# A fused decoder layer on one core: clearing the odd sums in three parts two steps later, and moving two more quarters of the K projection into the first three attention steps

## The chip, the cores and the metric

The kernel runs on one core of a Trainium2 chip. A core has a matrix engine (TensorE, PE in the profile, with PEld for its weight loads), a vector engine (VectorE, DVE), a scalar engine (ScalarE, ACT), a general engine (GpSimd, POOL), a queue engine (SyncE, SP) and 16 DMA engines. The metric is the device time of one execution in microseconds (us), smaller is better.

## The reference: what is computed

One decoder layer over 32 sequences (batches) of 128 rows and 256 features, float32:

```python
x = _layernorm(x + _L0_attn_ref(x, L0_attn_qkv_weights), axis=-1)          # causal self-attention, 16 heads of 16
x = _layernorm(x + _L0_xattn_ref(x, ctx_1024, ctx_1024, Wq, Wk, Wv), -1)   # retention with a decay mask on a context
x = _layernorm(x + _L0_ffn_ref(x, ...), axis=-1)                           # shared expert + 2 of 8 routed experts
```

In the self-attention, K is laid out in a peculiar way: `pre_k` of shape (rows, S, H, Dh) is turned to (Dh, S) per head after a plain reshape, so that one head's K mixes rows. The kernel therefore makes the K projection of eight sequences at a time (a group), writes it to device memory (`k_dram`) and reads each sequence's part back in the order in which the scores want it. In the routed part each row goes to the two experts with the largest gate probabilities, and the two results are added to the row.

## The kernel before

The engines run one program each, written out by hand, and meet at semaphores. There are three stages. The **front** (to about 28 us) loads x in four groups of eight sequences and makes the K projection. The **attention steps** follow: a function `step(n)` on each engine, for n from -2 on, where step n does the scores and the softmax of sequence n, the value product of sequence n-2, the cross part of n-3 and n-4, and the gate of n-5. Each step has the same work once the pipeline is full. The **tiles** (from about 470 us) run the routed experts over 71 tiles of 128 rows; each tile's result is added to one of two arrays in device memory, `totals[0]` (even tiles) and `totals[1]` (odd tiles), by an indirect DMA that adds. `totals[1]` has 33 x 128 rows of 256 floats and must be zero before the first odd tile.

What the change touches:

- **The K projection.** A group g has four quarters j. `project_k(g, j, bank)` on TensorE does a quarter as 8 matmuls into one PSUM bank (L735) and counts `k_made`; `out_k(g, j, bank)` on VectorE copies the bank to the group's place in `first_use` (L1304) and counts `kk_set`. Before the change the front holds groups 0 to 2 (12 quarters) and group 3 is spread: three quarters in step 0 and one in step 1. TensorE takes a bank again only after `kk_set` says that it was copied. The queue engine stores a finished group to `k_dram` (`store_k`, L453): group 0 in the front, groups 1 to 3 in its steps 1 to 3. K of sequence t comes back as eight loads in step t-1 (L477, `kp`).
- **What follows the front on TensorE:** `project(0)` (L768, L771: Q and V of sequence 0), the first masks (L778), then `scores(0)` (L791). `project(0)` waits for the x of sequence 0 (`xT_in`, issued at L467), for the small tables (`small_in`, L442 to L445) and others.
- **A step's inner order on TensorE (steps 0 to 2):** turning the probabilities of sequence n-1 (`turn_probs`, L803, four times, each needs the copy of the one before out of its bank: `out_probs`, on VectorE at L1434 or on ScalarE at L1112), the value product (`weigh`, L813), `scores(n)` (L791), `project(n+1)`. From step 3 on the cross part begins with L902, which needs the context of its sequence (`cT`, loaded at L486 in the step before).
- **The clearing.** GpSimd issues one DMA of zeros onto `totals[1]` at the start of its step 8 (L623), between two pieces of its own work: the root of the variance (L650) and the sum `kept` (L631). In steps 5 to 8 the queue engine also loads the routed experts' weights (L500, L503; four loads in a step). From step 12 on GpSimd sends each sequence's packets with two indirect DMAs a step (L637), after it has waited for the scores of the step.

Of the kernel before, what the change touches and what calls it, by code (L numbers as in the profile page):

```python
# [14 lines left out]
P = 128  # L15
# [22 lines left out]
EARLY = 4  # L38
SHARED_TURNS = 2
# [55 lines left out]
def decoder_kernel(nc, x, ctx_turned, wqkv, xwq, xwk, xwv, gate_w, gate_b, sw1, sb1, sw2, sb2,  # L95
                   rw1, biases, rw2, table_f32, table_bf16, x_turned, x_blocks, out):
    ctx = ExitStack()
    with ctx:
# [309 lines left out]
        def live(t):  # L408
            return 0 <= t < B
# [15 lines left out]
        def _(eng):  # L425
# [126 lines left out]
            eng.wait_ge(idle_sent, 48)  # L552
# [44 lines left out]
        def _(eng):  # L597
# [18 lines left out]
            def step(n):  # L616
# [5 lines left out]
                if n == 8:  # L622
                    eng.dma_start(totals[1][:, :].rearrange("(n p) d -> p n d", p=P),  # L623
                                  zeros[:, 0:D].unsqueeze(1).broadcast_to([P, B + 1, D])).then_inc(idle_sent, 16)
# [52 lines left out]
            eng.wait_ge(idle_sent, 48)  # L677
# [53 lines left out]
        def _(eng):  # L731
# [9 lines left out]
            for g in range(NG - 1):  # L741
                eng.wait_ge(xTu_in[g] if g else wk_in, 16)
                for j in range(4):
                    if g == 0:
                        eng.wait_ge(first_in[j], 16)
                    else:
                        eng.wait_ge(kk_set, (g - 1) * 4 + j + 1)
                    project_k(g, j, 4 + j)
            eng.wait_ge(xTu_in[NG - 1], 16)
            eng.wait_ge(ident_in, 16)  # L750
            eng.wait_ge(w_in, 32)
            eng.wait_ge(kk_set, 4 * NG - 5)
# [45 lines left out]
            def turn_probs(t, u):  # L798

                eng.wait_ge(expd, expd_count(t, u))  # L800
                after(eng, pT_set, t * 4 + u)
                for n in range(4):
                    mm = eng.transpose(PROBT[:, n * P:(n + 1) * P], prob[:, t % 2, 4 * u + n, :], ident)  # L803
                mm.then_inc(p_turned, 1)
# [69 lines left out]
            def step(n):  # L874
                if n == 1:
                    eng.wait_ge(kk_set, 13)
                if live(n - 1):
                    turn_probs(n - 1, 0)
                if n == 2:
                    eng.wait_ge(kk_set, 4 * NG)  # L880
# [4 lines left out]
                if n == 0:  # L885
                    eng.wait_ge(kk_set, 9)
                    project_k(NG - 1, 0, 4)
                if n == 1:
                    eng.wait_ge(kk_set, 14)
                    project_k(NG - 1, 3, 5)  # L890
# [51 lines left out]
                if live(n - 1):  # L942
                    turn_probs(n - 1, 2)
                t = n - 5
# [31 lines left out]
                if n == 0:  # L976
                    eng.wait_ge(kk_set, 12)
                    project_k(NG - 1, 1, 5)
                    project_k(NG - 1, 2, 7)
# [16 lines left out]
                if live(t):  # L996

                    eng.wait_ge(x1_set, t + 1)
                    after(eng, gc_set, n - 4)
                    for c in range(DC):  # L1000
                        mm = eng.transpose(TR[:, c * P:(c + 1) * P], x1[:, t % 2, c * P:(c + 1) * P], ident)
                    mm.then_inc(x1_turned, 1)
# [298 lines left out]
        def _(eng):  # L1301
# [5 lines left out]
            for g in range(NG - 1):  # L1307
                for j in range(4):
                    out_k(g, j, 4 + j)
# [158 lines left out]
            def step(n):  # L1468
# [7 lines left out]
                if n == 0:  # L1476
                    out_k(NG - 1, 0, 4)
                    lay_mask(1, 0)
                    lay_mask(1, 3)
                    out_k(NG - 1, 1, 5)  # L1480
                    out_k(NG - 1, 2, 7)
                if 0 < n <= SHARED_TURNS:
                    out_probs(n - 1, 1)
                if n == 1:
                    out_k(NG - 1, 3, 5)
                if n == 1:
                    out_probs(n - 1, 2)
                if live(t2):
                    eng.wait_ge(heads_turned, t2 + 1)
                    eng.reciprocal(rden[:, r2, :], HEADS[:, :, DH]).then_inc(den_set, 1)  # L1490
# [11 lines left out]
                if n == 2:  # L1502
                    out_probs(n - 1, 2)
# [253 lines left out]
```

## Time and profile before

| what | value |
|---|---|
| median of 3 runs | 726.83 us (725.86 to 726.84) |
| the profiled execution | 727.77 us, of which the span is 725.6 us |
| busy share of the span: PE, DVE, ACT, POOL | 94%, 67%, 66%, 47% |
| mean granted clock of TensorE | 0.986 |
| moved by DMA | 104.30 MB, mean 144 GB/s |

The profile is of one execution, which took 727.77 us, 2.17 us more than its span (start and end around it) and 0.94 us more than the median. Busy time says how much an engine worked, not whether the end waited for it; for that one reads the chain of work that ended last and the idle time before instructions. In the views, "PE ps L791" is TensorE writing to tile ps at line 791, and the bracket at the end of a row of the timeline is the idle time before it and what ended it. A row of windows has start:end and length, the busy time and instructions of PE, PEld, DVE, ACT and POOL, then the granted clock of TensorE (1.00 is 2.4 GHz, 0.50 is 1.2 GHz), the mean busy share of the DMA engines and GB/s.

### The profile page before, as it was taken

To read this page: it belongs to the slowest core of one execution; us is meant where nothing else is said; L and a number is where in the kernel's file an instruction comes from. 1 tells how busy PE (TensorE), PEld (TensorE's weight loads), DVE (VectorE), ACT (ScalarE), POOL (GpSimd) and SP (SyncE) were. 2 spreads that over 40 slices of the span, in tenths; PEclk is the share of its full clock that TensorE was granted. 3 is DMA by queue.
4 is the path that set the end of the run, shared out by engine and by line. 5 is a ranking of instruction groups with operands and counts; after the bars stand their busy time and mean duration, and the time that the engine had idled before them with its cause. 6 is when DMAs were issued, how large, how long until landed. Compare 5 with 4: busy or idle time off the path is not lost.

```text
span 725.6 us, 21537 instructions
## 1 busy us (share of the span) xinstructions
PE 682.8 (94%) x6174; PEld 589.5 (81%) x6175; DVE 489.3 (67%) x1563; ACT 478.6 (66%) x1319; POOL 341.7 (47%) x467
## 2 busy tenths in 40 slices
PE   7979999899999999999998889889999999999994
PEld 6868888788888888888887655779999999998653
DVE  3666877598888888888887456445555555555266
ACT  0278888588888888888885141356766666666246
POOL 1001334235454454554545446045656655556395
PEclk9999999899999999999999899999999999999998
DMA  8634469522332232323325224687777777776597
GB/s 314 216 131 138 140 198 308 194 61 76 91 94 70 89 100 75 107 80 107 112 80 173 76 72 147 186 220 132 139 133 142 135 139 134 141 135 133 118 349 264
DMA packets 93915, 104.30 MB, mean 144 GB/s; under 512 B 13168, under 2 KB 86640, under 8 KB 92944
## 3 DMA queue, kind: packets, MB, share of 16 engines
q1 hardware_dynamic: 78480, 79.43, 36.8%
q0 software_dynamic: 14656, 23.26, 16.8%
q8 instruction: 40, 0.66, 0.4%
q10 hardware_dynamic: 704, 0.66, 0.3%
q14 instruction: 35, 0.29, 0.1%
HBM read 62.21 MB, written 41.10 MB: 142 GB/s over the span
## 4 chain that ended last, share of the span: by engine, by line
PE 76%; DMA 6%; DVE 5%; SPq 4%; POOL 4%; issue 4%; ACT 1%; DVEq 0%; POOLq 0%; ACTq 0%
PE ps L1038 15%; PE ps L1047 8%; PE ps L803 6%; PE ps L902 5%; PE ps L791 5%; PE ps L768 4%; PE ps L813 4%; PE ps L905 4%; PE ps L735 4%; PE ps L926 4%; PE ps L771 4%; POOL first_use L711 2%; DMA xg<-sent 2%; PE ps L1025 2%; PE ps L823 2%
## 5 line engine op out<-in xcount | busy, mean ns | idle before, releaser
L1105 ACT ACTIVATE prob<-ps,nmax 128x128 f32<-128x128 f32 x512 | 146.5, 378 | 28.0 <-DVE nmax L1319 28.0
L1038 PEld LDWEIGHTS ps<-xgT,attn_only 128*128 128x128 f32 x1136 | 135.9, 192 | 7.4 <-DVE ghT L1600 1.8
L1038 PE MATMUL ps<-xgT,attn_only 128*128 128x128 f32 x1136 | 138.9, 276 | 1.1 <-ACT xgT L1217 1.1
L670 POOL DMA_INDIRECT total<-rot,result_row x71 | 112.4, 1583 | 35.3 <-issue 32.9
L1319 DVE TENSOR_REDUCE nmax<-ps 128x4 f32<-128x512 f32 x128 | 82.1, 685 | 17.9 <-PE ps L791 17.3
L1600 DVE SCALAR_TENSOR_TENSOR ghT<-ps,attn_only 128x128 f32<-128x128 f32 x142 | 43.3, 346 | 69.5 <-PE ps L1038 58.1
L613 POOL TENSOR_TENSOR rot<-products 128x128 f32<-128x128 f32 x128 | 61.1, 498 | 61.6 <-DVE products L1329 61.5
L1112 ACT COPY pT<-ps 128x512 f32<-128x512 f32 x124 | 74.3, 599 | 19.6 <-PE ps L803 15.3
L803 PE MATMUL ps<-tf,prob 128*128 128x128 f32 x512 | 78.5, 276 | 5.2 <-DVE pT L1434 4.2
L637 POOL DMA_INDIRECT sent<-packets,pos x64 | 63.4, 990 | 36.8 <-PE ps L791 22.6
L1047 PE MATMUL ps<-first_use,ghT 128*128 x284 | 74.5, 385 | 0.0
L803 PEld LDWEIGHTS ps<-tf,prob 128*128 128x128 f32 x512 | 59.1, 141 | 11.7 <-issue 4.1
L1225 ACT COPY attn_only<-first_use 128x512 f32 x71 | 44.0, 619 | 28.6 <-issue 28.6
L823 PE MATMUL ps<-prob,sw_sb 128*128 128x512 f32 x128 | 56.8, 594 | 0.0
L1217 ACT COPY xgT<-ps 128x256 f32<-128x256 f32 x71 | 26.4, 372 | 43.8 <-PE ps L1025 43.8
L1047 PEld LDWEIGHTS ps<-first_use,ghT 128*128 128x128 f32 x284 | 48.4, 190 | 5.4 <-issue 0.5
L1329 DVE TENSOR_TENSOR products<-ps,tf 128x256 f32<-128x256 f32 x128 | 46.4, 404 | 7.5 <-PE ps L905 2.3
L1589 DVE COPY attn_only<-first_use 128x512 f32 x71 | 31.2, 440 | 28.5 <-issue 28.0
L650 POOL TENSOR_TENSOR rstd<-mv,neg_half 128x1 f32<-128x1 f32 x32 | 17.6, 550 | 67.0 <-DVE mv L1337 67.0
L1211 ACT ACTIVATE attn_only<-ps,attn_only 128x128 f32<-128x128 f32 x142 | 44.1, 361 | 6.7 <-PE ps L1038 2.8
L658 POOL TENSOR_TENSOR weight<-weight_part,xg 128x1 f32<-128x1 f32 x71 | 13.3, 188 | 69.8 <-ACT rot L1231 52.9
L823 PEld LDWEIGHTS ps<-prob,sw_sb 128*128 128x128 f32 x128 | 23.9, 190 | 26.0 <-issue 25.6
(143 smaller groups left out, 1407.0 us busy)
## 6 DMA issues: line engine op xcount, KB each, us to landing
xg<-sent SPq DMA_DIRECT2D x71, 130.5 KB, 2.1
attn_only<-in_L_ffn_rb SPq DMA_DIRECT2D x71, 130.0 KB
first_use<-total SPq DMA_DIRECT2D x12, 512.0 KB, 8.5
total<-zeros POOLq DMA_DIRECT2D x1, 4224.0 KB, 18.0
k_dram<-first_use SPq DMA_DIRECT2D x4, 1024.0 KB, 5.1
attn_only<-in_x_turned SPq DMA_DIRECT2D x32, 128.0 KB, 2.3
attn_only<-k_dram SPq DMA_DIRECT2D x256, 16.0 KB
attn_only<-in_x SPq DMA_DIRECT2D x32, 128.0 KB, 2.7
```

Of the source, the lines that this page charges most:

```text
L613: eng.tensor_tensor(rot[:, t % 2, m + e, :], ra[:, t % 2, m + e, :], rb[:, t % 2, m + 1 - e, :], ALU.add).then_inc(done, 1)
L637: eng.indirect_dma_start(sent, bass.IndirectOffsetOnAxis(ap=pos[:, t, j:j + 1], axis=0), packets[:, t % SLOTS, :], None).then_inc(sent_in[ ...
L670: eng.indirect_dma_start(totals[slot % 2], bass.IndirectOffsetOnAxis(ap=result_row[:, slot:slot + 1], axis=0), yw[:, slot, :], None, compu ...
L803: mm = eng.transpose(PROBT[:, n * P:(n + 1) * P], prob[:, t % 2, 4 * u + n, :], ident)
L823: mm = eng.matmul(ps[:, bank + half, :].rearrange("p (b t) -> p b t", b=QB), sw1_sb[:, c, cols:cols + P], x2T4[:, q % EARLY, :, c, :], sta ...
L1038: mm = eng.matmul(ps[:, 2 * r + half, f * P:(f + 1) * P], w_now[:, r, c, cols:cols + P], xgT[:, r, c, :], start=(c == 0), stop=(c == DC - 1))
L1047: mm = eng.matmul(ps[:, 4 + r, 0:D], ghT[:, r, c, :], rw2_sb[:, bass.ds(e * (FFN // P * D) + c * D, D)], start=(c == 0), stop=(c == FFN // ...
L1105: ins = eng.activation(prob[:, t % 2, 4 * u + n, :], SCORE[u][:, n * P:(n + 1) * P], ACT.Exp, bias=nmax[:, t % 2, 4 * u + n:4 * u + n + 1])
L1112: eng.copy(pT[:, u, :, :].rearrange("p n t -> p (n t)"), PROBT).then_inc(pT_set, 1)
L1211: eng.activation(sil[:, r, f, :], ps[:, 2 * r, f * P:(f + 1) * P], ACT.Silu, bias=side[:, slot, f:f + 1]).then_inc(sil_set, 1)
L1319: eng.tensor_reduce(nmax[:, t % 2, 4 * u:4 * u + 4], SCORE[u].rearrange("p (h j) -> p h j", j=P), AX_X, ALU.max, negate=True).then_inc(max ...
L1329: eng.tensor_tensor(into[:, t % 2, m:m + 2, :], source, table[:, m:m + 2, :], ALU.mult).then_inc(done, 1)
```

## The change

First, the clearing of `totals[1]` is cut into three DMAs of 11 x 128 rows each, issued at the start of GpSimd's steps 10, 12 and 14, and no longer as one of 33 x 128 rows in step 8. Second, the front keeps 10 quarters of the K projection. The last two of group 2 and the four of group 3 are spread over steps 0, 1 and 2: three in step 0 as before (but other ones), two in step 1 (one before), one in step 2 (none before). Banks and counts of the waits are changed to fit.

```diff
+CLEARING = (10, 12, 14)
...
-                if n == 8:
-                    eng.dma_start(totals[1][:, :].rearrange("(n p) d -> p n d", p=P),
-                                  zeros[:, 0:D].unsqueeze(1).broadcast_to([P, B + 1, D])).then_inc(idle_sent, 16)
+                if n in CLEARING:
+                    many = (B + 1) // len(CLEARING)
+                    lo = CLEARING.index(n) * many * P
+                    eng.dma_start(totals[1][lo:lo + many * P, :].rearrange("(n p) d -> p n d", p=P),
+                                  zeros[:, 0:D].unsqueeze(1).broadcast_to([P, many, D])).then_inc(idle_sent, 16)
...
             for g in range(NG - 1):
                 eng.wait_ge(xTu_in[g] if g else wk_in, 16)
-                for j in range(4):
+                for j in range(4 if g < NG - 2 else 2):
...
-            eng.wait_ge(xTu_in[NG - 1], 16)
-            eng.wait_ge(kk_set, 4 * NG - 5)
+            eng.wait_ge(kk_set, 7)
...
                 if n == 1:
-                    eng.wait_ge(kk_set, 13)
+                    eng.wait_ge(kk_set, 12)
                 if live(n - 1):
                     turn_probs(n - 1, 0)
                 if n == 2:
-                    eng.wait_ge(kk_set, 4 * NG)
+                    eng.wait_ge(kk_set, 15)
...
                 if n == 0:
-                    eng.wait_ge(kk_set, 9)
-                    project_k(NG - 1, 0, 4)
+                    eng.wait_ge(kk_set, 8)
+                    project_k(NG - 2, 2, 7)
                 if n == 1:
+                    eng.wait_ge(kk_set, 11)
+                    project_k(NG - 1, 1, 7)
+                if n == 2:
                     eng.wait_ge(kk_set, 14)
-                    project_k(NG - 1, 3, 5)
+                    project_k(NG - 1, 3, 7)
...
                     turn_probs(n - 1, 2)
+                if n == 1:
+                    eng.wait_ge(kk_set, 13)
+                    project_k(NG - 1, 2, 5)
...
                 if n == 0:
-                    eng.wait_ge(kk_set, 12)
-                    project_k(NG - 1, 1, 5)
-                    project_k(NG - 1, 2, 7)
+                    eng.wait_ge(kk_set, 9)
+                    project_k(NG - 2, 3, 4)
+                    eng.wait_ge(xTu_in[NG - 1], 16)
+                    eng.wait_ge(kk_set, 10)
+                    project_k(NG - 1, 0, 5)
...
                 if n == 0:
-                    out_k(NG - 1, 0, 4)
+                    out_k(NG - 2, 2, 7)
                     lay_mask(1, 0)
                     lay_mask(1, 3)
-                    out_k(NG - 1, 1, 5)
-                    out_k(NG - 1, 2, 7)
+                    out_k(NG - 2, 3, 4)
+                    out_k(NG - 1, 0, 5)
                 if 0 < n <= SHARED_TURNS:
                     out_probs(n - 1, 1)
                 if n == 1:
-                    out_k(NG - 1, 3, 5)
-                if n == 1:
+                    out_k(NG - 1, 1, 7)
                     out_probs(n - 1, 2)
+                    out_k(NG - 1, 2, 5)
...
                 if n == 2:
+                    out_k(NG - 1, 3, 7)
                     out_probs(n - 1, 2)
```

In the changed kernel the same lines have other numbers: L735 is L739, L768 is L771, L803 is L806, L791 is L794 on TensorE; L1304 is L1317, L1319 is L1332, L1434 is L1447 on VectorE; L623 is L627 and L637 is L641 on GpSimd.

How TensorE's order changes, from behind `scores(1)` in step 1 to the turns of step 2 (a quarter is 4 matmuls in this order, and 8 records in the trace). Before:

```order
L735 MATMUL ps<-attn_only,first_use 128x256 x4
L803 MATMUL ps<-tf,prob 128x128 x12
L768 MATMUL ps<-attn_only 128x128 x4
L771 MATMUL ps<-attn_only 128x256 x2
L803 MATMUL ps<-tf,prob 128x128 x4
L813 MATMUL ps<-pT,va 32x128 x16
L791 MATMUL ps<-attn_only 128x128 x16
L912 MATMUL ps<-tf,oT 128x128 x4
L803 MATMUL ps<-tf,prob 128x128 x12
```

And now:

```order
L739 MATMUL ps<-attn_only,first_use 128x256 x4
L806 MATMUL ps<-tf,prob 128x128 x8
L739 MATMUL ps<-attn_only,first_use 128x256 x4
L806 MATMUL ps<-tf,prob 128x128 x4
L771 MATMUL ps<-attn_only 128x128 x4
L774 MATMUL ps<-attn_only 128x256 x2
L806 MATMUL ps<-tf,prob 128x128 x4
L816 MATMUL ps<-pT,va 32x128 x16
L794 MATMUL ps<-attn_only 128x128 x16
L739 MATMUL ps<-attn_only,first_use 128x256 x4
L918 MATMUL ps<-tf,oT 128x128 x4
L806 MATMUL ps<-tf,prob 128x128 x12
```

In step 1 the quarter behind the scores is still there (now another one), and a second quarter stands ahead of the last turn. In step 2 a quarter stands between the scores and the turning of the heads (L912, now L918), ahead of the three turns of the step.

VectorE's order in steps 1 and 2, from the maxima of step 1 (nmax) to the second copy of probabilities in step 2. "first_use<-ps" is `out_k`, "pT<-ps" is `out_probs`. Before:

```order
L1319 TENSOR_REDUCE nmax<-ps 128x4 [waits scored] x4
L1434 COPY pT<-ps 128x512 [waits p_turned]
L1304 COPY first_use<-ps 128x2x256 [waits k_made]
L1434 COPY pT<-ps 128x512 [waits p_turned]
L1428 CAST ps<-tb 128x512 [waits expd] x2
L1319 TENSOR_REDUCE nmax<-ps 128x4 [waits expd,scored] x3
L1434 COPY pT<-ps 128x512 [waits heads_made,p_turned]
L1490 RECIPROCAL rden<-ps 128x16 [waits heads_turned]
L1495 TENSOR_TENSOR att<-ps,rden 128x256 [waits den_set]
L1434 COPY pT<-ps 128x512 [waits heads_made,p_turned]
```

And now:

```order
L1332 TENSOR_REDUCE nmax<-ps 128x4 [waits scored] x4
L1447 COPY pT<-ps 128x512 [waits p_turned]
L1317 COPY first_use<-ps 128x2x256 [waits k_made]
L1447 COPY pT<-ps 128x512 [waits p_turned]
L1317 COPY first_use<-ps 128x2x256 [waits k_made]
L1441 CAST ps<-tb 128x512 [waits expd] x2
L1332 TENSOR_REDUCE nmax<-ps 128x4 [waits expd,scored] x3
L1447 COPY pT<-ps 128x512 [waits heads_made,p_turned]
L1503 RECIPROCAL rden<-ps 128x16 [waits heads_turned]
L1508 TENSOR_TENSOR att<-ps,rden 128x256 [waits den_set]
L1317 COPY first_use<-ps 128x2x256 [waits k_made]
L1447 COPY pT<-ps 128x512 [waits heads_made,p_turned]
```

One copy of a quarter was added behind the second pT of step 1, and one ahead of the second pT of step 2.

GpSimd's order where a part of the clearing now stands, in step 12 (step 14 reads the same, step 10 has no indirect DMAs):

```order
L654 TENSOR_TENSOR rstd<-mv,neg_half 128x1 [waits mv2_set]
L627 DMA total<-zeros 128x11x256
L635 TENSOR_TENSOR kept<-packets,sb_sb 128x256 [waits x2_set]
L641 DMA sent<-packets,pos 34688x261 [waits scored,pos_set]
L641 DMA sent<-packets,pos 34688x261
L615 TENSOR_TENSOR rot<-products 128x128 [waits scx_made,pk_set]
```

Before, the one clearing stood at the same place of step 8:

```order
L650 TENSOR_TENSOR rstd<-mv,neg_half 128x1 [waits mv2_set]
L623 DMA total<-zeros 128x33x256
L631 TENSOR_TENSOR kept<-packets,sb_sb 128x256 [waits x2_set]
L613 TENSOR_TENSOR rot<-products 128x128 [waits scx_made,pk_set]
```

The part is ahead of `kept` and of the two indirect DMAs of the step.

## Rows read from the trace of the kernel before

**Rows 1.** The page: the chain that ended last, by engine, share of the span

```profile
PE 76%; DMA 6%; DVE 5%; SPq 4%; POOL 4%; issue 4%; ACT 1%; DVEq 0%; POOLq 0%; ACTq 0%
```

**Rows 2.** Timeline of TensorE, steps 8 to 10 (start, length, line, idle before)

```profile
113.73 1.17 PE L791 MATMUL ps<-attn_only 32*128 32x128 f32 x32
...
125.50 1.18 PE L791 MATMUL ps<-attn_only 32*128 32x128 f32 x32 [0.58 <-issue]
129.59 2.07 PE L902 MATMUL ps<-attn_only 128*128 128x128 f32 x8 [2.91 <-DMA attn_only<-in_ctx]
...
142.52 1.17 PE L791 MATMUL ps<-attn_only 32*128 32x128 f32 x32
143.63 1.16 PE L902 MATMUL ps<-attn_only 128*128 128x128 f32 x8
```

**Rows 3.** Windows of 2 us: busy times, then granted clock, DMA share, GB/s

```profile
116.00:118.00 2.00, 2.00 (x16) 1.85 (x16) 1.51 (x5) 1.94 (x9) 0.00 (x0) 1.00 1.00 329
...
130.00:132.00 2.00, 2.00 (x10) 1.91 (x10) 0.00 (x0) 0.00 (x0) 0.00 (x0) 0.50 1.00 354
```

**Rows 4.** Windows of whole steps: step 7 with weight loads, step 14 without

```profile
102.55:113.73 11.18, 11.14 (x134) 9.74 (x131) 8.83 (x25) 9.45 (x29) 3.92 (x8) 1.00 0.63 202
...
187.22:198.33 11.11, 10.91 (x134) 9.79 (x130) 9.82 (x32) 9.45 (x29) 5.75 (x9) 1.00 0.33 85
```

**Rows 5.** The page: the clearing's issue, KB, us to landing

```profile
total<-zeros POOLq DMA_DIRECT2D x1, 4224.0 KB, 18.0
```

**Rows 6.** Timeline of GpSimd: its DMA issues and a send of step 14

```profile
113.41 1.92 POOL L623 DMA_DIRECT2D total<-zeros  x1
...
189.29 1.02 POOL L637 DMA_INDIRECT sent<-packets,pos  x1 [1.02 <-PE ps L791]
```

**Rows 7.** Timeline of the queue engine: loads in steps 8 and 10

```profile
112.55 7.71 SPq L477 DMA_DIRECT2D attn_only<-k_dram  x8
120.30 1.25 SPq L486 DMA_DIRECT2D attn_only<-in_ctx  x1
...
141.33 4.62 SPq L477 DMA_DIRECT2D attn_only<-k_dram  x8
```

**Rows 8.** Timeline of TensorE from the front to step 2

```profile
21.21 7.07 PE L735 MATMUL ps<-attn_only,first_use 128*128 128x256 f32 x32
28.12 1.05 PE L768 MATMUL ps<-attn_only 128*128 128x128 f32 x8
...
30.83 1.18 PE L791 MATMUL ps<-attn_only 32*128 32x128 f32 x32
...
43.97 0.63 PE L803 MATMUL ps<-tf,prob 128*128 128x128 f32 x4 [0.93 <-DVE pT L1434]
45.49 0.63 PE L803 MATMUL ps<-tf,prob 128*128 128x128 f32 x4 [0.89 <-DVE pT L1434]
...
51.06 0.60 PE L803 MATMUL ps<-tf,prob 128*128 128x128 f32 x4
53.12 0.63 PE L803 MATMUL ps<-tf,prob 128*128 128x128 f32 x4 [1.46 <-DVE pT L1434]
54.62 0.63 PE L803 MATMUL ps<-tf,prob 128*128 128x128 f32 x4 [0.87 <-DVE pT L1434]
```

**Rows 9.** Timeline of VectorE in steps 1 and 2

```profile
43.74 1.08 DVE L1304 COPY first_use<-ps 128x512 f32<-128x512 f32 x1
...
52.29 0.68 DVE L1434 COPY pT<-ps 128x512 f32<-128x512 f32 x1
...
53.78 0.69 DVE L1434 COPY pT<-ps 128x512 f32<-128x512 f32 x1 [0.19 <-PE ps L803]
```

**Rows 10.** The queue engine's x loads (L467): issue, and us to landing

```profile
L467 SPq DMA_DIRECT2D attn_only<-in_x_turned x2: 432/432/432, 19.9 to 20.4; - x2
...
DMA to landing us min/median/max: 5.3/5.4/5.4
```

**Rows 11.** Window of 1 us while K of sequence 0 lands

```profile
26.00:27.00 1.00, 1.00 (x6) 0.90 (x5) 0.41 (x1) 0.00 (x0) 0.00 (x0) 1.00 0.09 19
```

More of the change, by code:

```diff
@@ L38 @@
 EARLY = 4
+CLEARING = (10, 12, 14)
+assert (B + 1) % len(CLEARING) == 0
 SHARED_TURNS = 2
@@ L551, in _ @@
             eng.wait_ge(zeros_put, 16 * NE)
-            eng.wait_ge(idle_sent, 48)
+            eng.wait_ge(idle_sent, 16 * (2 + len(CLEARING)))
             def load(i, slot):
@@ L676, in _ @@
                 eng.wait_ge(x2_stored[r], 16 * (B - EARLY * QB) // 2)
-            eng.wait_ge(idle_sent, 48)
+            eng.wait_ge(idle_sent, 16 * (2 + len(CLEARING)))
             eng.wait_ge(kept_stored, 16 * EARLY)
@@ L998, in step @@
                     eng.wait_ge(x1_set, t + 1)
+                    if t == 0:
+                        eng.wait_ge(kk_set, 4 * NG)
                     after(eng, gc_set, n - 4)
@@ L1307, in _ @@
             for g in range(NG - 1):
-                for j in range(4):
+                for j in range(4 if g < NG - 2 else 2):
                     out_k(g, j, 4 + j)
```

## The prediction

> **What bounds the kernel now.** I read the chain of work that ended last first: TensorE has 76% of it [rows 1]. So time comes out only where TensorE waits or runs slowly, and the rest of the reading looks for such places near the two edits.
>
> The first is in steps 8 and 9. In TensorE's timeline scores(8) begins at 113.73, scores(9) at 125.50 and scores(10) at 142.52 [rows 2]: two steps take 28.79 us. Whole steps around them take 11.18 and 11.11 us [rows 4]. The excess is 28.79 - 11.18 - 11.11 = 6.50 us. Of it 0.58 + 2.91 = 3.49 us are idle time, ahead of scores(9) and ahead of the cross part, where the context's load had not landed. The other 3.0 us are slow running: the cross part's first group takes 2.07 us there and 1.16 in the next step [rows 2], and a window just behind the wait has a granted clock of 0.50, that is 1.2 GHz of 2.4, against 1.00 before [rows 3]. TensorE had sat idle 2.91 us ahead of that.
>
> Who made the load late? The clearing: 4224 KB, 18.0 us from issue to landing [rows 5], issued at 113.41 [rows 6], so the DMA engines were full until 131.4 (share 1.00, 329 GB/s) [rows 3]. The queue engine took 7.71 us to issue the eight K loads, against 4.62 in step 10, and came to the context only at 120.30 [rows 7]; TensorE could take it only at 129.59.
>
> The second place is the start. The front's last four quarters take 7.07 us of pure work at full rate, then project(0) begins at 28.12 and scores(0) at 30.83 [rows 8]. In steps 1 and 2 TensorE has idle gaps of 0.93, 0.89, 1.46 and 0.87 us, all for VectorE's copy of turned probabilities [rows 8]. These 4.15 us are the only room in which moved quarters could be hidden.
>
> **The change, part by part.** *The clearing leaves step 8.* With it goes the whole excess, if nothing else makes that load late: step 7 has the same weight loads as step 8, a DMA share of 0.63 and no excess [rows 4]. Term: -6.5. I take the slow clock with the wait, since its rows are at 0.50 only behind the wait.
>
> *Three parts arrive.* Each has 1408 KB. By 4224 KB in 18.0 us it needs 6.0 us, shared with other traffic; that was at 329 GB/s in all, and step 14 now moves only 85 GB/s, share 0.33 [rows 3 to 5]. The part starts, as the whole did, while the K loads are issued. If K loads are again issued over as much as 7.71 us instead of 4.62, the context's is issued as late in the step as it was in step 8; but the part has then about landed, and TensorE wants the context only 129.59 - 2.91 - 120.30 = 6.4 us later [rows 2, 7]. No wait. Bounds of each part: 0 below; above, a third of the old excess, 2.2 us. I take 0, as the row of the step with share 0.63 is nearer: with a part, step 14 moves 85 GB/s x 11.1 us + 1.44 MB = 2.4 MB, about step 7's 202 x 11.18 = 2.3 MB.
>
> *Issue on GpSimd.* A part costs GpSimd at most the whole's 1.92 us [rows 6], in front of `kept` and of the sends. In step 14 the sends wait 1.02 us for the scores [rows 6]; what is above that (at most 0.9) delays the rotation, whose result TensorE reads a step later. Cost 0. The two further issues have no waiter on TensorE. The last part is issued in step 14, and the first odd tile adds hundreds of us later.
>
> *The front ends two quarters earlier.* A quarter is (28.12 - 21.21)/4 = 1.73 us [rows 8], so TensorE is free 3.46 us earlier, at 24.66. But project(0) needs x of sequence 0: issued at 19.9, landing in 5.3 to 5.4 [rows 10], at 25.3. Its issue hangs on the first store of K, which doesn't move. So project(0), and with it scores(0), starts 28.12 - 25.3 = 2.8 earlier. Step 0 has as many quarters as before, at the same places. Then scores(0) needs K of sequence 0. Its eight loads are issued behind x, from about 20.8 on; at 4.62 us for eight [rows 7] the last goes out at 25.4, and if it lands as slowly as x, it is there at 30.8, and nothing of the 2.8 is left. The other bound: the engines are nearly idle from 26 to 27, share 0.09 [rows 11], so those loads had landed, and scores(0) can start at 28.0. I take that one, since it is a row on the loads themselves. Term: -2.8 (ends: -3.46 if x is in too, 0 if K lands as slowly as x).
>
> *Step 1 gets a quarter* ahead of the last turn, where TensorE idled 0.89 us [rows 8]. 1.73 - 0.89 = +0.8. VectorE's copy of it (1.08) [rows 9] lies behind the last copy of the step, where it next waits for scores(2). Term: +0.8.
>
> *Step 2 gets a quarter* behind the scores, ahead of the turn at 51.06. That turn ended at 51.66, 0.6 us before VectorE came to copy it, at 52.29 [rows 8, 9], so the copy starts 1.73 - 0.6 = 1.1 later. Then VectorE copies the quarter itself ahead of the second probabilities: 1.08, less the 0.19 that it idled there [rows 9]. TensorE's last turn waits for that copy. Term: 1.1 + 0.9 = +2.0. Here the quarter costs all it saved in front: TensorE's gaps of 1.46 and 0.87 [rows 8] were VectorE's work, and VectorE gets more of it.
>
> K projection: -2.8 + 0.8 + 2.0 = 0.0. Ends: -2.0 (step 2's quarter hides in TensorE's gaps after all) to +2.8 (K of sequence 0 is late). Sum: -6.5 + 0.0 = **-6.5**. The profiled execution took 727.77, so it would be 721.3; the runs' median is 0.94 below it, 726.83, which gives **720.3**.
>
> **A rule against the change.** The granted clock is 0.50 behind 2.91 us of idle time [rows 3], and 1.00 over whole steps that have no such wait [rows 4]. The Trainium skill, "TensorE: Matmul & The Clock Gate", section "HAM oscillation", says that a wait for a DMA that comes back again and again makes the array start cold each time, so that the cost of the clock is paid as often as there are waits. By that, three short waits would be dearer than one, if the parts make any; what it would give is the last rival. The trace agrees on the fall of the clock behind the one long wait.
>
> **The rivals.**
> 1. *The K quarters are hidden.* TensorE idled 4.15 us in steps 1 and 2, more than the 3.46 moved there. Against it: the gaps are VectorE's work, and step 2 adds a copy to it. The time then: -6.5 - 2.8 + 0.8 = -8.5, so 718.3.
> 2. *Parts still leave some waits*, because loads of K issued behind a part come late in each of three steps, without a fall of the clock: three times 0.58, the wait ahead of scores(9) [rows 2]. -6.5 + 1.7 = -4.8, so 722.0. For it: the K loads are issued together with the part, as then.
> 3. *The K move loses.* The queue engine's chain did not move while TensorE's did, so scores(0) waits for K of sequence 0: up to -6.5 + 2.8 = -3.7, 723.1; half of that, 721.7, is its middle. Against it: the quiet engines at 26 us [rows 11].
> 4. *Slower.* Each part makes the context's load late as the whole did, in steps 10, 12 and 14, and the clock falls each time: 3 x 6.50 in place of 6.50 is +13.0, so 739.8. It decides from the point where a part keeps the context's load from landing for more than a step, as 18.0 us did; 6.0 us end well ahead of that, so little speaks for it.
> 5. *The change doesn't do what it says*: the late load of step 8 was late for the weights of that step and not for the clearing. Then steps 8 and 9 keep their 6.5 and the result is 726.8. Against it: step 7 with the same loads is whole [rows 4].
>
> **How the numbers follow.** The forecast has 0.62; rival 1 0.12, rival 2 0.10, rival 3 0.09, rival 4 0.03, rival 5 0.04. The forecast's own spread is about 1 us to either side, 719.3 to 721.3. The range reaches over rival 1, rival 2 and most of rival 3: 718.2 to 722.6. About 0.2%, or 1.5 us, is what a measurement of this kernel can tell from no change. Faster than 725.4: the forecast and rivals 1 to 3, 0.93. Within 0.2%: rival 5, 0.04. Slower: rival 4, 0.03.
>
> **What the profile would show.** Scores begin every 11.1 to 11.2 us from step 7 to step 11, with a clock of 1.00 throughout and no idle time on TensorE for the context. Three clearing DMAs of 1408 KB, each landing in some 5 to 7 us. Project(0) starts at about 25.4, ahead of it a short wait for a DMA; scores(0) near 28.1. Step 1 and step 2 are longer by 0.8 and 2.0, so that scores(3) begins where it began before; in step 2 the last turn still waits for VectorE. It would be wrong if a part of the clearing holds up loads in step 10, 12 or 14, or if VectorE is not the one that TensorE waits for in step 2.

## The result and the profile after

The changed kernel takes 723.39 us (median of 22 runs, 720.01 to 728.08) against 728.26 for the kernel before on the same chip (22 runs, 724.45 to 730.97). The ratio is 0.9949, 95% interval 0.9932 to 0.9966. That is 3.7 us less (2.5 to 5.0), a gain clear of the noise but small, half a per cent, where 6.5 us were forecast. The time is 0.8 us above the top of the range. Part of that is the start of the sum: the three runs that gave 726.83 lay low, and 22 runs give 728.26. But 3.7 less than 726.83 is 723.1, which is outside too. The profiled execution took 723.76, its span is 721.7.

The page of the changed kernel: the span, the chain that ended last, and the issue of the three parts (count, KB, us to landing).

```profile
span 721.7 us, 21540 instructions
...
PE 78%; DVE 5%; DMA 5%; POOL 4%; issue 4%; SPq 3%; ACT 1%; DVEq 0%; POOLq 0%; ACTq 0%
...
total<-zeros POOLq DMA_DIRECT2D x3, 1408.0 KB, 8.0
```

TensorE's timeline in steps 8 to 10 of the changed kernel, which answers to [rows 2]:

```profile
114.98 1.17 PE L794 MATMUL ps<-attn_only 32*128 32x128 f32 x32
116.09 1.16 PE L908 MATMUL ps<-attn_only 128*128 128x128 f32 x8
...
126.10 1.17 PE L794 MATMUL ps<-attn_only 32*128 32x128 f32 x32
127.20 1.16 PE L908 MATMUL ps<-attn_only 128*128 128x128 f32 x8
...
137.21 1.17 PE L794 MATMUL ps<-attn_only 32*128 32x128 f32 x32
```

A step's length is the time from its scores to the next step's. Both waits are gone, and the cross part's first group takes 1.16 us where it took 2.07. Steps 8 and 9 last 22.23 us; before they lasted 28.79, so 6.56 went. The windows of whole steps 8 (weights alone), 10 and 12 (a part of the clearing each), which answer to [rows 3] and [rows 4]:

```profile
114.98:126.10 11.12, 10.92 (x135) 9.79 (x131) 8.73 (x25) 9.58 (x29) 3.66 (x7) 1.00 0.66 202
...
137.21:148.32 11.11, 10.92 (x134) 9.79 (x130) 9.83 (x32) 9.46 (x29) 4.71 (x8) 1.00 0.59 192
159.50:170.60 11.10, 10.90 (x142) 9.79 (x130) 9.53 (x28) 9.55 (x30) 6.60 (x10) 1.00 0.65 209
```

A step with a part has a DMA share of 0.59 or 0.65, no more than one with weight loads (0.66), a clock of 1.00 and a length of 11.11 or 11.10 us. The queue engine's loads in step 10 of the changed kernel (to [rows 7]):

```profile
136.02 6.40 SPq L479 DMA_DIRECT2D attn_only<-k_dram  x8
142.46 0.43 SPq L488 DMA_DIRECT2D attn_only<-in_ctx  x1
```

The K loads still take 6.40 us to issue beside a part (7.71 beside the whole, 4.62 alone), but the context goes out at 142.46, some 7 us before step 11's cross part.

TensorE from the front to step 2 (to [rows 8]):

```profile
21.82 3.62 PE L739 MATMUL ps<-attn_only,first_use 128*128 128x256 f32 x16
25.52 1.13 PE L771 MATMUL ps<-attn_only 128*128 128x128 f32 x8
...
28.31 1.17 PE L794 MATMUL ps<-attn_only 32*128 32x128 f32 x32
...
36.98 1.17 PE L794 MATMUL ps<-attn_only 32*128 32x128 f32 x32
...
47.37 1.17 PE L794 MATMUL ps<-attn_only 32*128 32x128 f32 x32
48.48 1.99 PE L739 MATMUL ps<-attn_only,first_use 128*128 128x256 f32 x8
...
52.22 0.63 PE L806 MATMUL ps<-tf,prob 128*128 128x128 f32 x4 [0.88 <-DVE pT L1447]
54.34 0.63 PE L806 MATMUL ps<-tf,prob 128*128 128x128 f32 x4 [1.49 <-DVE pT L1447]
54.80 1.72 PE L771 MATMUL ps<-attn_only 128*128 128x128 f32 x8
56.32 1.91 PE L774 MATMUL ps<-attn_only 128*128 128x256 f32 x4
...
59.99 1.17 PE L794 MATMUL ps<-attn_only 32*128 32x128 f32 x32
```

Project(0) starts at 25.52 and scores(0) at 28.31, 2.52 earlier than before. No wait stands ahead of project(0) in this profile, but x landed at about the same time as the front ended: the same kernel in e1, and three of the five others with this front, show a wait for it of 0.22 to 0.54 us. In e1:

```profile
25.09 1.13 PE L771 MATMUL ps<-attn_only 128*128 128x128 f32 x8 [0.54 <-DMA attn_only<-in_x_turned]
```

Step 1 takes 10.39 (9.74 before), step 2 takes 12.62 (9.41 before): +0.65 and +3.21. The two groups behind the gap of 1.49 take 1.72 and 1.91 us, where they took about 1.06 and 1.03 elsewhere. Windows of the changed kernel there:

```profile
52.00:54.00 2.00, 0.63 (x4) 0.42 (x4) 1.97 (x5) 1.06 (x4) 0.00 (x0) 1.00 1.04 311
54.00:56.00 2.00, 1.66 (x11) 1.69 (x12) 1.90 (x6) 0.59 (x1) 0.53 (x1) 0.75 0.38 131
56.00:58.00 2.00, 2.00 (x7) 1.56 (x7) 1.61 (x4) 1.14 (x4) 0.05 (x1) 0.50 0.03 8
```

TensorE is busy 0.63 of 2 us while it waits for VectorE, and behind that the granted clock is 0.75 and 0.50. VectorE of the changed kernel in step 2 (to [rows 9]):

```profile
51.38 0.69 DVE L1447 COPY pT<-ps 128x512 f32<-128x512 f32 x1 [0.89 <-PE ps L806]
...
52.61 1.06 DVE L1317 COPY first_use<-ps 128x512 f32<-128x512 f32 x1
53.52 0.68 DVE L1447 COPY pT<-ps 128x512 f32<-128x512 f32 x1
```

By this one pair of profiles the change would be worth 5.6 us up to scores(31) (371.83 against 377.42) and 3.9 at the end (721.7 against 725.6).

### The profile page after: what moved, and what is told of

Its sections match the earlier page's. It is cut to its first block, busy times and chain, and to the rows that moved or that the text cites. A ratio compares the mean times of both kernels' runs of the same rounds, so it can differ in the third digit from the quotient of the medians.

```text
span 721.7 us, 21540 instructions
## 1 busy us (share of the span) xinstructions
PE 683.2 (95%) x6174; PEld 588.5 (82%) x6175; DVE 489.2 (68%) x1563; ACT 478.9 (66%) x1319; POOL 343.1 (48%) x469
## 4 chain that ended last, share of the span: by engine, by line
PE 78%; DVE 5%; DMA 5%; POOL 4%; issue 4%; SPq 3%; ACT 1%; DVEq 0%; POOLq 0%; ACTq 0%
PE ps L1051 15%; PE ps L1060 8%; PE ps L806 6%; PE ps L908 5%; PE ps L794 5%; PE ps L816 4%; PE ps L771 4%; PE ps L739 4%; PE ps L911 4%; PE ps L774 4%; PE ps L932 4%; DMA xg<-sent 3%; POOL first_use L715 2%; PE ps L1038 2%; PE ps L826 2%
## 5 line engine op out<-in xcount | busy, mean ns | idle before, releaser
L1332 DVE TENSOR_REDUCE nmax<-ps 128x4 f32<-128x512 f32 x128 | 82.2, 685 | 17.7 <-PE ps L794 17.0
L806 PE MATMUL ps<-tf,prob 128*128 128x128 f32 x512 | 77.9, 275 | 4.4 <-DVE pT L1447 3.3
L641 POOL DMA_INDIRECT sent<-packets,pos x64 | 63.6, 993 | 35.6 <-PE ps L794 20.9
L806 PEld LDWEIGHTS ps<-tf,prob 128*128 128x128 f32 x512 | 58.7, 140 | 11.0 <-issue 4.9
```

The costliest lines, as they stand in the source:

```text
L641: eng.indirect_dma_start(sent, bass.IndirectOffsetOnAxis(ap=pos[:, t, j:j + 1], axis=0), packets[:, t % SLOTS, :], None).then_inc(sent_in[ ...
L1332: eng.tensor_reduce(nmax[:, t % 2, 4 * u:4 * u + 4], SCORE[u].rearrange("p (h j) -> p h j", j=P), AX_X, ALU.max, negate=True).then_inc(max ...
```

## The experiments

Sixteen runs were made, each with a profile, so that the stages can be told over many executions. Some repeat a kernel. Each ratio is to the kernel before on the same chip; e8, e10, e11 and e16 have one execution each and no ratio. "Old order" is TensorE's order of K quarters in the kernel before, "half clock" a granted clock of 0.50, and "excess" what steps 8 to 11 take above the 44.70 us that they take after the change.

**e1, the changed kernel again; e2, the clearing in parts alone** (the kernel before with GpSimd's lines of the change); **e3, the K quarters alone.**

```diff
# e3, in the changed kernel
-CLEARING = (10, 12, 14)
+CLEARING = (8,)
```

> The changed kernel once more, for a second profile and to share its chip with the single parts. Theory 1 (the clearing gives 6.5 us; the K move costs about 1.3 us, of which some 1.6 us is a stretch of half clock in step 2): ratio to before about 0.993; if the half clock in step 2 belongs to this order of work, this profile has it again (step 2 of about 12.6 us against 9.4 before). Rival (the half clock in step 2 was chance): step 2 of about 11.0 to 11.4 us and a clock of 1.00 there.

> Only the clearing is changed (three parts in steps 10, 12 and 14); the K projection stays as before. Theory 1: steps 8 and 9 take 22.2 us and not 28.8, so 6.5 us less than before, ratio about 0.991, and 1 to 1.5 us faster than the full change. Rival (the K move is neutral, and something behind the attention gives back what the result lacks): the same time as the full change, about 0.995.

> Only the K projection is moved; the clearing stays whole in step 8. Theory 1: scores(0) 2.5 us earlier, step 1 +0.65, step 2 +3.2, so scores(3) 1.3 us later than before: ratio 1.001 to 1.002. Rival (K move neutral as predicted): 1.000, scores(3) where it was; in that case step 2 has no half clock.

Ratios: e1 0.9935 (0.9907 to 0.9962), e2 0.9949 (0.9927 to 0.9971), e3 0.9999 (0.9975 to 1.0023). The 0.991 expected of e2 did not come; its rival's 0.995 did. All of the gain that can be told is the clearing's; moving the K quarters alone gives no difference (the interval reaches 1.8 us to either side). In e2 steps 8 to 11 take 44.69 us, as after the change (44.70), so the parts cost TensorE nothing. In e3, with the whole in step 8, they take 49.30: an excess of 4.60 and not 6.56. The repeats of the kernel before (e10, e16) show that this size differs between executions of one kernel: 5.89 and 4.40. Step 2 takes 12.33 in e1 and 12.62 in e3.

**e4, step 2's quarter in the gap**: TensorE does it while VectorE copies the first turned probabilities.

```diff
-                if n == 2:          # behind scores(n)
-                    eng.wait_ge(kk_set, 14)
-                    project_k(NG - 1, 3, 7)
...
+                if n == 2:          # behind turn_probs(n - 1, 1)
+                    eng.wait_ge(kk_set, 14)
+                    project_k(NG - 1, 3, 7)
```

> The full change, but in step 2 TensorE does its quarter of K behind the turn of the second four heads, and not ahead of it and of the turning of the heads; VectorE's order is as in the full change. Theory 1 (TensorE's quarter made VectorE idle 0.9 us, and long gaps on TensorE afterwards brought the half clock): step 2 takes about 10.4 us, 1.0 less from the order and 1.2 to 1.6 less from the clock, total about 2 us faster than the full change. Rival (VectorE's copy of the quarter alone sets step 2): step 2 unchanged at 12.6, or only the clock's part of it gone.

TensorE of e4 in step 2:

```profile
47.13 1.17 PE L794 MATMUL ps<-attn_only 32*128 32x128 f32 x32
...
49.38 1.89 PE L739 MATMUL ps<-attn_only,first_use 128*128 128x256 f32 x8
51.11 0.60 PE L806 MATMUL ps<-tf,prob 128*128 128x128 f32 x4
53.12 0.63 PE L806 MATMUL ps<-tf,prob 128*128 128x128 f32 x4 [1.41 <-DVE pT L1447]
53.58 1.06 PE L771 MATMUL ps<-attn_only 128*128 128x128 f32 x8
54.48 1.03 PE L774 MATMUL ps<-attn_only 128*128 128x256 f32 x4
```

Ratio 0.9897 (0.9868 to 0.9926). One gap of 1.41 is left, the groups behind it take 1.06 and 1.03, and the step 10.02 us instead of 12.62. The last turn begins 5.99 us behind the scores (6.97 after the change): 1.0 us is order, and 1.6 us is the clock, in this one profile.

**e5, the whole in step 10; e7, three parts in step 8.** Is it the place beside the weight loads, or the length of the one DMA?

```diff
# e5, in e2
-CLEARING = (10, 12, 14)
+CLEARING = (10,)
# e7, in e2
-                if n in CLEARING:
+                if n == 8:
...
+                    for lo in range(0, (B + 1) * P, many * P):
```

> K projection as before; the clearing is one DMA of 4224 KB again, but in step 10, where no weights are loaded. Theory 1 (it is the length of one transfer that holds up the context's load, the weights matter little): steps 10 and 11 take 4 to 6.5 us more than two whole steps, with a stretch of half clock; total about as before, ratio 0.998 to 1.000. Rival (it was the meeting with the weight loads of step 8, so that the move alone cures it): no excess, total as with three parts, ratio about 0.994 to 0.995. Beside it, tiles 10 to 70: 176.2 to 176.8 us if what stretches them is the later clearing, 175.1 to 175.7 if it is the number of clearing DMAs.

> K projection as before; three clearing DMAs of 1408 KB, all issued one behind the other in step 8. Theory 1 (the bytes in a row count, not the number of DMAs): steps 8 and 9 have the excess of about 5 to 6.5 us as before, ratio about 1.000. Rival (cutting alone helps, since the queue engine's loads slip in between): the excess falls below 3 us. Beside it, tiles 10 to 70: 176.2 to 176.8 us if the number of clearing DMAs stretches them, 175.1 to 175.7 if not.

TensorE of e5 in step 11, and then of e7 in step 9:

```profile
147.43 1.17 PE L795 MATMUL ps<-attn_only 32*128 32x128 f32 x32
150.57 1.16 PE L906 MATMUL ps<-attn_only 128*128 128x128 f32 x8 [1.97 <-DMA attn_only<-in_ctx]
```

```profile
126.33 1.17 PE L795 MATMUL ps<-attn_only 32*128 32x128 f32 x32 [0.84 <-issue]
130.24 2.07 PE L906 MATMUL ps<-attn_only 128*128 128x128 f32 x8 [2.73 <-DMA attn_only<-in_ctx]
```

Neither text on e5 was right: an excess came, but without the half clock. The whole away from the weights still makes the context late, by 1.97 us, but the clock stays up (1.16 behind the wait): the excess is 46.73 - 44.70 = 2.0 us, all of it the wait. That is one profile; whether the clock falls behind such a wait in other executions was not measured. Three parts issued together are the whole again: excess 6.63, ratio 1.0012 (0.9982 to 1.0042). So the gain has two parts: away from the weight loads, and steps between the pieces. The ratio of e5 is 0.9949 (0.9921 to 0.9976), the same as e2's: the 2 us lie within the two intervals, so only the trace shows them.

**e6 and e12, the quarter in the gap and copied by ScalarE; e8, the quarter where the change has it, but copied behind the second probabilities.**

```diff
# e6, e12, in e4
-                    out_k(NG - 1, 3, 7)      # VectorE, step 2
# and on ScalarE, between exps(n, 3) and out_probs(n - 1, 3)
+                if n == 2:
+                    eng.wait_ge(k_made, 16)
+                    eng.copy(kk_of(NG - 1).rearrange("p (a u) -> p u a", u=NU)[:, 6:8, :],
+                             ps[:, 7, :].rearrange("p (u a) -> p u a", u=2)).then_inc(kk_set, 1)
# e8, in the changed kernel, VectorE, step 2
-                    out_k(NG - 1, 3, 7)
                     out_probs(n - 1, 2)
+                    out_k(NG - 1, 3, 7)
```

> The full change, with two edits in step 2: TensorE's quarter of K behind the turn of the second four heads, and its copy done by ScalarE ahead of its own last copy of probabilities, where it waited 1.94 us, in place of VectorE. Theory 1: with both the quarter and the copy in idle time, step 2 takes 9.4 to 9.7 us as before the change, at full clock, so scores(3) comes 1.9 to 2.3 us earlier than before and the total is 8.5 us under it, ratio about 0.989. Rival (ScalarE is as tight as VectorE there): step 2 at 10.0 or more as with the move on TensorE alone.

> The full change, but in step 2 VectorE copies the quarter of K behind the second copy of probabilities and not ahead of it; TensorE's order is that of the full change. Theory 1 (VectorE's copy is what TensorE's last turn waits for, and the two gaps together bring the half clock): the last turn waits about 0.4 us in place of 1.49, no half clock in step 2, the step takes 11.0 to 11.4 us. Rival (TensorE's quarter ahead of the second turn alone sets the step): step 2 stays above 12 us.

> The version with TensorE's quarter of step 2 in the gap and its copy on ScalarE, once more, for a second profile and a second interval. If the first was no chance draw: steps 0 to 2 take 28.5 to 28.6 us at full clock again (the change itself had 31.4 to 31.7 in three profiles), steps 8 to 11 take 44.7, and the ratio to before is 0.989 to 0.993. Rival (the half clock in step 2 comes at random in every order of work, as it did in one profile of the kernel before): steps 0 to 2 take about 30 us in this profile.

TensorE of e6, and then of e8, in step 2:

```profile
52.49 0.63 PE L806 MATMUL ps<-tf,prob 128*128 128x128 f32 x4 [0.87 <-DVE pT L1451]
52.95 1.06 PE L771 MATMUL ps<-attn_only 128*128 128x128 f32 x8
```

```profile
52.17 0.63 PE L806 MATMUL ps<-tf,prob 128*128 128x128 f32 x4 [0.87 <-DVE pT L1447]
53.67 0.63 PE L806 MATMUL ps<-tf,prob 128*128 128x128 f32 x4 [0.88 <-DVE pT L1447]
54.13 1.06 PE L771 MATMUL ps<-attn_only 128*128 128x128 f32 x8
...
56.81 0.44 PE L1014 MATMUL ps<-tf,x 128*128 128x128 f32 x2 [0.76 <-DVE x L1538]
```

In e8 the copy no longer stands ahead of the last turn, the gap shrinks from 1.49 to 0.88 (0.4 was expected) and the clock stays up, but `x` is late by 0.76: 11.31 us. In e6 and e12 step 2 takes 9.49 and 9.48 and is as short as without a quarter. Ratios: e6 0.9921 (0.9894 to 0.9948), e12 0.9895 (0.9858 to 0.9933); e8's one run took 723.51. These kernels are the best: e4, e6 and e12 beat the kernel before and, by the middle of their intervals, the change; only e4's interval is clear of the change's.

**e9, two small DMAs more; e10, the kernel before; e11, e2 again.** In e2 and after the change the stretch of the tiles (from the tenth to the seventieth) was 0.8 to 1.0 us longer than before. Do more DMAs on GpSimd's queue do that?

```diff
# e9, in the kernel before
+                if n in (12, 14):
+                    lo = (n - 12) // 2 * P
+                    eng.dma_start(spare[lo:lo + P, :], zeros[:, 0:D]).then_inc(idle_sent, 16)
```

> The kernel before, with two more small DMAs (128 KB of zeros each onto unused rows of device memory) issued by GpSimd in steps 12 and 14; the clearing stays whole in step 8. Theory (the tiles' stretch comes with two more DMAs on GpSimd's queue, wherever they are and however large): tiles 10 to 70 take 176.2 to 176.8 us in place of 175.1 to 175.8, and the total is about 1 us above before, ratio 1.001. Rival (it comes with the clearing of the odd sums in parts): tiles 10 to 70 at 175.1 to 175.8, ratio 1.000.

> The kernel before once more, for a second profile of it. If the parts of the time that the change does not touch are the same from one execution to another, scores(31) begins 346.6 us behind scores(0), tile 0 some 84.3 us behind scores(31), and tiles 10 to 70 take 175.1 to 175.8 us. If they vary by 1 to 2 us, then that is what stands between the 5.6 us gained by scores(31) and the measured ratio.

> Only the clearing in three parts once more, for a second profile, since the first was of the fastest of its executions. Up to scores(31) it should be the same as the first (6.5 us less in steps 8 and 9, and no excess); tiles 10 to 70 at 176.2 to 176.8. An execution of 724 to 725 us should show its longer time behind scores(31): in the passage to the tiles, in tiles 0 to 10 or at the end.

The theory fell: that stretch is 176.35 in e9 and 177.64 in e11, but 176.58 in e10, the kernel before (175.74 in its first profile). e9's ratio is 1.0003 (0.9979 to 1.0026). The same profiles showed something else. TensorE of e10 in step 2, in the old order:

```profile
53.38 0.63 PE L803 MATMUL ps<-tf,prob 128*128 128x128 f32 x4 [1.45 <-DVE pT L1434]
54.88 1.09 PE L803 MATMUL ps<-tf,prob 128*128 128x128 f32 x4 [0.87 <-DVE pT L1434]
55.76 1.92 PE L768 MATMUL ps<-attn_only 128*128 128x128 f32 x8
57.47 1.28 PE L771 MATMUL ps<-attn_only 128*128 128x256 f32 x4
```

The same gaps as in [rows 8], 1.45 and 0.87, and this time the clock falls behind them. The kernel before pays this too, in some executions.

**e13 to e16: is the gain given back behind scores(31)?** With the three parts alone steps 8 to 11 are 4.4 to 6.6 us shorter than with the whole, but the ratio of e2 gives only 3.7. Theories A to D are in the text of e13 and e14.

```diff
# e13, in e2; spare has as many rows as totals[1]
+                if n == 8:
+                    eng.dma_start(spare[:, :].rearrange("(n p) d -> p n d", p=P),
+                                  zeros[:, 0:D].unsqueeze(1).broadcast_to([P, B + 1, D])).then_inc(idle_sent, 16)
# e14, in e2: in project(t), ahead of its own six matmuls
+                for _ in range(3 if t == 10 else 0):
...              # the same six matmuls, without a signal
```

> Three parts of the clearing in steps 10, 12 and 14, and besides them GpSimd writes as many zeros (4224 KB) as the old clearing into a spare array at the old place in step 8: work that the reference does not ask for. Steps 8 and 9 should again be some 5.7 us longer (mean of five profiles of kernels with the whole there). The question is the stretch behind scores(31): 348.6 us in the mean of four profiles with the clearing whole in step 8 (347.7 to 349.8), 351.4 in the mean of nine with it moved (349.0 to 353.2). Theory A, a stall in step 8 makes the later stretch short: it is short again here, and the mean span is that of the kernel before (725 to 726). Theory B, writing the real array later makes the later stretch long: it stays long, some 351.4, and the mean span is 2.7 above that of the kernel before. Theory C, the difference of the two groups of profiles is chance: the mean span is that of the three parts alone (722.0) and 5.7, 727.7, and the stretch is anywhere from 348 to 353.

> Three parts of the clearing in steps 10, 12 and 14, and in step 9 TensorE does the projection of sequence 10 four times instead of once (three times of work whose result is overwritten with the same values), about 3 x 1.8 = 5.4 us of work without idle time. Theory D, the stretch behind scores(31) depends on when it begins: it begins as late as in the kernel before, is short, and the mean span is 725 to 726. Theories A, B and C: busy work changes nothing later, so the mean span is 722.0 + 5.4 = 727.4.

> Three parts in steps 10, 12 and 14 and nothing else, a third time. If the stretch behind scores(31) is longer with the clearing moved, it is above 349.8 again (it was 349.0 and 353.2) and the ratio is near 0.995, not the 0.991 that the traces up to scores(31) would give. If that was chance, the stretch is as often near 348 as near 353, and the ratio comes nearer 0.992.

> The kernel before, for one more profile of the stretch behind scores(31): 347.7 to 349.8 if kernels with the clearing in step 8 have it short, anywhere up to 353 if not. Steps 8 to 11 take 49 to 51.5 us.

Ratios: e13 1.0020 (0.9994 to 1.0045), e14 1.0027 (1.0009 to 1.0045), e15 0.9967 (0.9939 to 0.9995). All eighteen profiles in the order in which scores(31) begins (us; "whole" means 4224 KB written in step 8):

```
kernel  scores(31)  behind it      kernel  scores(31)  behind it
e6        368.89     349.91        e15       373.42     350.18
e4        369.12     352.38        e13       375.45     349.65  whole
e12       369.18     352.92        e3        376.86     348.64  whole
e2        370.27     349.03        before    377.42     348.18  whole
e8        370.52     351.08        e16       377.72     348.38  whole
e11       370.87     353.23        e9        377.84     352.46  whole
e1        371.28     351.12        e7        377.86     347.74  whole
after     371.83     349.87        e14       378.10     347.90
e5        373.33     352.27        e10       378.32     349.78  whole
```

The stretch behind scores(31) is 349.3 us in the mean of the seven with the whole in step 8 and 350.9 in the eleven others. The line through the eighteen falls by 0.29 us for each us that scores(31) begins later (correlation -0.58; 7 of 1,000 random orders of the same numbers are as steep). So the profiles give back some 1.6 us on the way to the end.

The experiments do not say through what. B is not favoured: e14, with the clearing moved and the time filled with work, has a short stretch, 347.90. A is not borne out: e13, with its stall, has 349.65 and a mean span of 726.4, between A and C, and e9 has 352.46. D has its direction right by its profile, but not by its time. The mean spans that the theories named assume the 725.8 that the kernel before had in the first runs; it has 724.9 beside e14, whose ratio is 1.0027, and its interval is above the 1.000 that D gives and holds the 1.002 of the others. So C, chance alone, is not excluded.

Where the 1.6 us lie can be read: 0.5 before the first tile and 1.1 from there on. A part of it is the clock. The time lost to it behind scores(31), one less the granted clock times the length of each 1 us window, is 5.6 to 6.6 us in six of the seven with the whole (9.8 in e9), 5.7 to 9.6 in the ten with it moved and no filler, and 4.4 in e14. In the mean of the seven and of the eleven that is 6.5 and 7.0, so the clock is 0.4 of the 1.6, and the rest has no cause found.

## Why the prediction was wrong in size, part by part

**The clearing leaves step 8, -6.5.** Right in mechanism: waits, slow rows and the late context all went, and e7 brought them back. But less than half of it is the clearing by itself: in step 10, away from the weight loads, the whole cost 2.0 us (e5). Wrong in size. The rows of [rows 2] came from an execution near the top: steps 8 to 11 of the seven profiles with 4224 KB in step 8 (before, e3, e7, e9, e10, e13, e16) take 51.26, 49.30, 51.33, 49.60, 50.59, 49.14 and 49.10, mean 50.05, against 44.68 to 44.72 in those with the parts in steps 10, 12 and 14 and no filler. The term is -5.35.

What made it too large is above all the slow running, which the prediction put at 3.0 us. Summed over windows of 1 us, the clock costs 3.4 us in steps 8 to 11 of before, e7 and e10 and 1.7 us in the other four; the waits differ less. A window of 12 us around the wait in the kernel before, first in the profile that the prediction read, then in e16 (granted clock 0.72 and 0.86):

```profile
126.00:138.00 12.00, 8.83 (x65) 7.92 (x60) 4.70 (x12) 4.57 (x15) 1.70 (x4) 0.72 0.89 306
```

```profile
126.00:138.00 12.00, 9.48 (x110) 8.25 (x108) 6.51 (x18) 6.63 (x19) 2.74 (x6) 0.86 1.02 356
```

Of the 3.35 us that the clearing gained by leaving the weight loads, an estimate from these rows and e5 is that 2.4, the mean of the seven, are clock.

**Three parts, 0.** Right: 11.11 us a step at a clock of 1.00. The parts land in 7.8 to 8.0 us in this profile (medians of 6.8 to 8.3 in the others with parts in steps 10, 12 and 14) and not in 5 to 7, but nothing on TensorE waited for it. Rival 4, which the prediction's paragraph on the rule calls the last and which the clock rule of the Trainium skill ("TensorE: Matmul & The Clock Gate", "HAM oscillation") stood beside, did not come: there was no wait to come back. Rival 2's waits of 0.58 did not come either, nor rival 5.

**The front, -2.8.** Right: -2.52 in the pair of profiles; in the mean 28.22 in three against 30.94 in the eleven of the old order, -2.7. The forecast bound, the landing of `x`, is there as a wait in e1 and e3 (0.54 and 0.22 us). In the profile after, the front's last two quarters began later, at 21.82, and ended at 21.82 + 3.62 = 25.44, when `x` was in. K of sequence 0 was in each time, so rival 3 did not come.

**Step 1, +0.8**: +0.65 in the pair. Right. Against the mean of the old order it is +0.35, because two of its eleven profiles lose the clock in step 1 (11.41 us for 9.74).

**Step 2, +2.0.** The mechanism named is there: VectorE's first copy begins 4.01 us behind the scores (3.04 before), and the last turn waits for VectorE, 6.97 behind them (5.37 before): +1.60 for the +2.0. The other +1.6 is a half clock behind the gaps of 0.88 and 1.49, which the working put at nothing: it took gaps of this length to cost only themselves. Against the profile of before the term is +3.2. Against the mean it is smaller, because the old order also loses the clock there, in five of its eleven profiles (9.4 us six times, 10.83 or 11.00 five times, mean 10.1; 12.5 in the three of the change's order): +2.4. Rival 1, a hidden quarter, was wrong for this order and right for e6.

**K projection, 0.0.** Right in the mean: scores(3) begins at 59.80 (three profiles) against 59.76 (eleven), and e3's ratio is 0.9999.

**The sum, -6.5.** The measured -3.7 can be made up of -5.35 for the clearing, +0.05 for the quarters (-2.7, +0.35 and +2.4), and +1.6 for what is given back behind scores(31). Two steps of the prediction failed. The clearing's term was -6.5 and measured -5.35, shown by seven profiles. By itself this would have left the time in the range: 726.83 - 5.3 = 721.5. The second is that the working let every us saved early arrive at the end, a term put at nothing without a reason; the profiles show +1.6 there, a difference between two groups of profiles, with its cause open. That the three add up to -3.7 so closely is luck, as the interval of the ratio is 2.5 us wide. The runs say the same as the ratio: e2's mean span over twelve runs is 722.0 against 725.8 for 25 runs of before, -3.8, and by its mean granted clock over them (0.9895 against 0.9868) 2.0 us of it is clock, where the prediction counted 3.0 in steps 8 and 9 alone. e15, the same kernel as e2, gained less (0.9967, which is 2.4 us).

## What to carry to other kernels

Take the size of a stall from several executions before you count it: here one profile showed 6.56 us and the mean was 5.35, and the sum of the stages of one pair of profiles was off by some 2 us. A bulk write like this clearing belongs where no bulk loads are, and in pieces with a step between them: here the first saved about three fifths (by one profile, e5), the second the rest. When a piece of matmul work is moved to a later step, put it into the gap behind the instruction that the other engine still has to serve, and give its copy to the engine that TensorE doesn't wait for: the same quarter cost 3.2, 0.6 or 0.1 us in step 2 of three orders, against the 9.4 us of the old order at full clock.

## What the runs showed of the hardware

- The granted clock fell to 0.50 behind two short gaps, 0.88 and 1.49 us, in three of three profiles with the change's order. Behind gaps of 1.45 and 0.87 in the old order it fell in five of eleven, with the same rows before it (in two of these five in step 1 as well). Two gaps of 0.87 and 0.88 (e8) or one of 1.97 (e5) left it at 1.00, each in one profile.
- Between scores(31) and the first tile the same instructions took 83.45 to 87.33 us in the eighteen profiles. The clock is a part of that: 84.25 to 84.27 us in five profiles and 85.1 to 85.2 in six, with 3.4 us lost to the clock in each, some 85.7 in four with 5.1 lost, 87.33 in one with 6.8 lost, and 83.45 in one with 1.7 lost. But e12 took 86.84 with only 1.7 lost.
- The clock is much of why single executions of one kernel lie up to 8 us apart. In the 22 runs of the changed kernel the time lost to it, by each run's span and mean granted clock, goes from 5 us (clock 0.993) to 12 us (0.983), and its correlation with the span is 0.84.
- A DMA's time to land depended on its neighbours: 1408 KB took 6.8 to 8.7 us alone in a step (ten profiles) and 7.5 to 14.8 when three stood in a row in step 8 (e7).
